# The experts' down projection in three fp32r products instead of plain f32

## The reference

```
for e in range(E):                                  # 8 experts
    g = xf @ wg[e].T                                # 256 -> 384
    u = xf @ wu[e].T                                # 256 -> 384
    y = jax.nn.silu(g) * u @ w_down[e].T            # 384 -> 256, "down"
    out = out + comb[:, e:e + 1] * y                # comb: 2 of 8 not zero
```

## Time and profile before

| | before |
|---|---|
| median of three runs | 576.96 us |
| span of the profiled execution (first to last instruction) | 575.3 us |
| PE, DVE, ACT, POOL busy | 482.2, 287.6, 204.3, 161.4 us |
| 39 tiles, from the fourth up block (385.66 us) to the last (534.82 us) | 149.16 us in 36 steps |

### The profile page before, as it was taken

How to read it: one execution, slowest core, us unless ns; L and a number is a source line. 1 busy time by engine, 2 the same in 40 slices (tenths; PEclk the granted TensorE clock), 3 DMA queues, 4 the chain that set the end, 5 groups by cost and what they waited for, 6 DMA issues and landing times.

```text
span 575.3 us, 9801 instructions
## 1 busy us (share of the span) xinstructions
PE 482.2 (84%) x2849; PEld 312.9 (54%) x2850; DVE 287.6 (50%) x590; ACT 204.3 (36%) x415; POOL 161.4 (28%) x186
## 2 busy tenths in 40 slices
PE   4536896999978997998879999279999999999890
PEld 2314442474424642473353555268888888888650
DVE  6746373647555572646544666114343433434357
ACT  1213464544536163544663444013232323232110
POOL 7004342312324043311211287601222222221200
PEclk9957799999979998998999999779999999999995
DMA  8759229191837539290207422212222222221168
GB/s 267 171 54 112 65 54 144 39 174 38 122 72 111 137 65 129 53 159 2 83 3 291 173 86 93 98 40 64 57 66 62 65 64 64 64 64 55 37 191 255
DMA packets 48193, 56.66 MB, mean 98 GB/s; under 512 B 10640, under 2 KB 43472, under 8 KB 47536
## 3 DMA queue, kind: packets, MB, share of 16 engines
q1 hardware_dynamic: 44768, 47.10, 38.0%
q0 software_dynamic: 3408, 9.34, 4.5%
HBM read 27.05 MB, written 16.59 MB: 76 GB/s over the span
## 4 chain that ended last, share of the span: by engine, by line
PE 53%; DMA 12%; DVE 9%; issue 7%; ACT 7%; POOL 6%; SPq 5%; ACTq 0%; POOLq 0%; DVEq 0%
PE set_b L889 9%; DMA attention<-attention 7%; POOL x_by_slot L555 6%; PE set_a L873 6%; PE set_a L592 5%; PE set_a L875 5%; PE set_a L874 5%; PE set_b L622 5%; SPq L357 5%; ACT attention L987 4%; PE set_a L643 3%; PE set_b L612 3%; DVE attention L1190 3%; PE set_a L798 2%; PE set_b L881 2%
## 5 line engine op out<-in xcount | busy, mean ns | idle before, releaser
L1190 DVE TENSOR_REDUCE attention<-set_a 128x2 f32<-128x1024 f32 (+2 forms) x96 | 96.7, 1042 | 57.5 <-PE set_a L594 55.6
L987 ACT ACTIVATE attention<-set_b 128x512 f32<-128x512 f32 (+1 forms) x176 | 87.5, 565 | 69.4 <-PE set_b L612 68.7
L592 PE MATMUL set_a<-attention 96*128 96x512 bf16 (+3 forms) x256 | 67.8, 330 | 32.7 <-DMA attention<-attention 26.0
L564 POOL DMA_INDIRECT y_by_choice<-moe,e_dst x39 | 37.2, 955 | 140.4 <-DVE moe L1372 131.8
L521 POOL TENSOR_SCALAR_AFFINE_SELECT attention<-attention 128x512 f32<-128x512 f32 x64 | 39.8, 634 | 116.3 <-ACT attention L987 116.2
L592 PEld LDWEIGHTS set_a<-attention 96*128 96x128 bf16 x256 | 26.7, 104 | 80.1 <-issue 46.2
L612 PE MATMUL set_b<-attention 99*128 99x512 bf16 (+3 forms) x256 | 60.8, 312 | 11.0 <-ACT attention L987 6.0
L1358 DVE TENSOR_TENSOR moe<-set_a,moe 128x384 f32<-128x384 f32 x39 | 21.7, 557 | 92.0 <-ACT moe L1075 92.0
L889 PE MATMUL set_b<-w_down,moe 128*128 x234 | 60.3, 388 | 1.1 <-DVE moe L1372 1.1
L1075 ACT ACTIVATE moe<-set_a 128x384 f32<-128x384 f32 x39 | 19.1, 490 | 116.7 <-PE set_a L875 116.7
L873 PE MATMUL set_a<-wup_hi,e_xT_hi 128*128 x156 | 57.1, 366 | 1.6 <-DVE e_xT_lo L1353 1.2
(11 more groups left out here) (152 smaller groups left out, 691.3 us busy)
## 6 DMA issues: line engine op xcount, KB each, us to landing
attention<-attention SPq DMA_DIRECT2D x96, 128.0 KB, 5.7
wup<-in_wupT SPq DMA_DIRECT2D x2, 3072.0 KB, 14.1
x_by_slot<-attention SPq DMA_DIRECT2D x13, 387.0 KB, 7.4
moe<-x_by_slot SPq DMA_DIRECT2D x39, 128.0 KB, 2.0
moe<-y_by_choice SPq DMA_DIRECT2D x16, 256.0 KB, 3.8
attention<-in_ctxT SPq DMA_DIRECT2D x7, 512.0 KB, 5.9
w_down<-in_wdnT SPq DMA_DIRECT2D x3, 1024.0 KB, 8.6
x_res<-in_x SPq DMA_DIRECT2D x4, 512.0 KB, 7.2
```

The costliest lines, as they stand in the source:

```text
L592: mm(dst, qstack[0:ROWS, g // 2, h, k * P:w], kstack[0:ROWS, g // 2, h, 0:w], start=True, stop=False)
L987: nc.scalar.activation(pT[k][:, h:h + heads, :], bank(par)[:, 0:heads * (S - k * P)], ACT.Exp).then_inc(b_free, 1)
L1190: v.tensor_reduce(dst, src, AX.X, ALU.max, negate=True).then_inc(a_free, 1)
```

## The change

Both operands of the down projection are split into a high part (a copy to fp32r) and a low part (the rest, in fp32r), and each f32 product becomes three fp32r products. The low part of the weights takes the place of the f32 weights in memory, the high part stands where the attention's buffers were. The weights are split once, after the third shared batch; the hidden rows in every step, where DVE gets a new instruction `hidden_lo`. `e_hTr`, for which PE waits, is now raised by DVE.

```
-        wdn = sb("w_down", [P, M, E * D])
+        with nc.sbuf_tensor("w_down", [P, M, E * D], F32) as wdn:
+            pass
+        wdn_lo = sb("w_down_lo", [P, M, E * D], F32R)
...
+        wdn_hi = sb("w_down_hi", [P, M, E * D], F32R)
...
                 for m in range(M):
-                    last = mm(Bk[:, 2, 0:D], e_hT[:, a, m, :], wdn[:, m, bass.ds(e * D, D)],
-                              start=m == 0, stop=m == M - 1)
+                    cols = bass.ds(e * D, D)
+                    dst = Bk[:, 2, 0:D]
+                    mm(dst, e_hT_hi[:, a, m, :], wdn_hi[:, m, cols], start=m == 0, stop=False)
+                    mm(dst, e_hT_hi[:, a, m, :], wdn_lo[:, m, cols], start=False, stop=False)
+                    last = mm(dst, e_hT_lo[:, a, m, :], wdn_hi[:, m, cols], start=False, stop=m == M - 1)
...
+            pe.wait_ge(dn_lo, M)
...
# ACT, after the last silu of the third shared batch
+            for m in range(M):
+                copy(wdn_hi[:, m, :], wdn[:, m, :]).then_inc(dn_hi, 1)
...
-                copy(e_hT[:, a], Bk[:, 1, 0:M * P].rearrange("p (c n) -> p c n", c=M)).then_inc(e_hTr, 1)
+                copy(e_hT_hi[:, a], Bk[:, 1, 0:M * P].rearrange("p (c n) -> p c n", c=M)).then_inc(e_hThi, 1)
...
# DVE
+            for m in range(M):
+                dve.wait_ge(dn_hi, m + 1)
+                v.tensor_tensor(wdn_lo[:, m, :], wdn[:, m, :], wdn_hi[:, m, :], ALU.subtract).then_inc(dn_lo, 1)
+
+            def hidden_lo(t, a):
+                dve.wait_ge(e_hThi, t + 1)
+                v.tensor_tensor(e_hT_lo[:, a], Bk[:, 1, 0:M * P].rearrange("p (c n) -> p c n", c=M),
+                                e_hT_hi[:, a], ALU.subtract).then_inc(e_hTr, 1)
...
             hidden(1, 1)
+            hidden_lo(0, 0)
             rows_lo(2, 0)
...
                 t = 2 * i + 1
+                hidden_lo(t, 1)
                 rows_lo(t + 2, 1)
                 result(t - 1, 0, i, wait)
                 hidden(t + 2, 1)
+                hidden_lo(t + 1, 0)
                 rows_lo(t + 3, 0)
...
+            hidden_lo(NT - 2, 1)
             result(NT - 3, 0, (NT - 3) // 2)
+            hidden_lo(NT - 1, 0)
...
-    nc = bacc.Bacc("TRN2", target_bir_lowering=False, num_devices=1)
+    nc = bacc.Bacc("TRN2", target_bir_lowering=False, num_devices=1, dynamic_dma_scratch_size=4096)
```

More of the change, by code:

```diff
@@ L125, in build @@
         MOE = 39 * KB
+        with nc.sbuf_tensor("e_hT_hi", [P, 2, M, P], F32R) as e_hT_hi, \
+                nc.sbuf_tensor("e_hT_lo", [P, 2, M, P], F32R) as e_hT_lo:
+            pass
         moe = sb("moe", [P, MOE])
@@ L194, in build @@
         parts_of(moe, C * N)
+        part(2 * 2 * M * P)
         e_x = part(2 * D).rearrange("p (a d) -> p a d", a=2)
@@ L197, in build @@
         e_h = part(2 * HALF).rearrange("p (a d) -> p a d", a=2)
-        e_hT = part(2 * M * P).rearrange("p (a c n) -> p a c n", a=2, c=M)
         e_y = part(2 * D).rearrange("p (a d) -> p a d", a=2)
@@ L253, in build @@
         up_hi, up_lo, wts_ready, e_xhi = (sem(n) for n in ("up_hi", "up_lo", "wts_ready", "e_xhi"))
-        e_xt, e_xTr, e_up, e_sgr, e_hr, e_ht, e_hTr, e_yf, e_yr = (sem(n) for n in
-            ("e_xt", "e_xTr", "e_up", "e_sgr", "e_hr", "e_ht", "e_hTr", "e_yf", "e_yr"))
+        e_xt, e_xTr, e_up, e_sgr, e_hr, e_ht, e_hThi, e_hTr, e_yf, e_yr = (sem(n) for n in
+            ("e_xt", "e_xTr", "e_up", "e_sgr", "e_hr", "e_ht", "e_hThi", "e_hTr", "e_yf", "e_yr"))
+        dn_hi, dn_lo = sem("dn_hi"), sem("dn_lo")
         y_in = [sem(f"y_in{i}") for i in range(NYB)]
```

## The result

| | before | after |
|---|---|---|
| median (range), beside each other | 576.74 us (576.19 to 578.29) | 591.0 us (590.55 to 592.43) |
| span of the profiled execution | 575.3 us | 590.7 us |
| PE, DVE, ACT, POOL busy | 482.2, 287.6, 204.3, 161.4 us | 481.0, 307.3, 209.7, 163.7 us |

The ratio of after to before is 1.0242, with a 95% interval of 1.0218 to 1.0265: slower by 2.4%. The forecast was 590.0 us.

What follows compares the result with a forecast made beforehand. DVE's `e_xT_lo`, not PE, was taken to set each up block's start. 11.0 us in the loop and 2.1 in the scatter on a span of 575.3 make 588.4, with 1.7 to the median 590.0 us; range 585 to 596.

Steps and rivals of the forecast that it cites:

- the larger term: Expert loop: `hidden_lo` on DVE delays each up block by 0.30 us, 11.0 us of the 13.1 added.
- What bounds the loop: Expert loop: DVE's `e_xT_lo` sets the up block's start, 0.14 us after its end; the down block is hidden.
- Part 1: Down block: nine fp32r products at 0.12 take 1.08 us, 0.22 less than now; hidden, so the gain is 0.
- Part 2: DVE in each step: `hidden_lo` ahead of `rows_lo` adds 0.30 us, 37 times: 11.0 us, at most 16.9.
- Part 3: Splitting the weights: hidden for ACT and DVE, but DVE's subtractions slow POOL's scatter by 2.1 us (1.6 to 2.65).
- full blocking: Skill's rule, not adopted: three new DVE pieces would hold POOL up to 6.8 us, some 5 above the term.
- Part 4: The rest: smaller descriptor memory costs 0, or 66 us if only one DMA fits; clock's mean effect 0.
- One sign of the list: Expert loop, if right: a window of PE about 86% busy, with a wait on DVE before the up block.
- PE's stream sets the loop: Rival: the up block waits for the down block, 39 blocks save 0.22 us each; 570.5 us, faster; chance 0.06.
- The rival with more exposed: DVE's instructions do not overlap (16.9), PE's sequencer is late (1.8), scatter pays 2.65: 21.4 us, 598; chance 0.10.
- that with less: Rival: something in a step gives back half of the 0.30; 5.5 + 2.1 makes 584.5 us; chance 0.07.
- mostly not: Scatter: +0.40 us per POOL DMA beside DVE pieces of 1.69 was read as mostly not full blocking.

Runs made afterwards that it cites:

- e4: Changed kernel without `hidden_lo`, with three high by high products in the down block in place of nine: 582.17 us, ratio 1.007.
- e2: Kernel before, f32 products kept, with `hidden_lo` alone added on DVE and PE's wait moved to it: 586.53 us, ratio 1.0158.
- e9: Kernel before with the rows of tile t + 2 taken first on PE, ACT and DVE, f32 products kept: 570.51 us, ratio 0.9875.
- e3: Changed kernel without `hidden_lo`, all nine products kept, the third reading the high hidden rows: 583.46 us, ratio 1.0086.
- e7: Changed kernel with one swap on DVE, `rows_lo` ahead of `hidden_lo`: 582.73 us, ratio 1.0108.
- e8: Changed kernel with the rows of tile t + 2 first on PE, ACT and DVE, and descriptor memory 8192: 574.23 us, ratio 0.9937.
- e5: Changed kernel with descriptor memory of 8192 in place of 4096: 592.66 us, ratio 1.0246.
- e6: e5 without DVE's subtractions for the low down weights, the middle product reading the high weights: 587.9 us, one run.
- e1: Kernel before with the descriptor memory alone cut to 4096: 580.02 us, ratio 1.0029.
- e11: e9 with the split of the up weights in 16 pieces of 768 instead of 8 of 1536: 568.76 us, ratio 0.9846.
- e10: e5 with DVE's subtraction for the low down weights in six pieces of 1024 instead of three of 2048: 592.53 us, ratio 1.0245.

## Why the prediction was right

The prediction gave 590.0 us, 13.1 of them added; 591.0 was measured, 14.3 more than before. The mechanism of the larger term is shown. That the total is within 1 us is in part luck, as the sum below shows. By its own parts:

- **What bounds the loop: shown.** The constant 0.14 behind `e_xT_lo`, in steps whose down blocks end at different times, was the reason. It held after (443.30 to 443.44), with three products (e4) and with f32 products (e2), and over all 37 up blocks of each. It went when the order made PE's stream the later one (e9), and in every second step of the kernels with nine products and an earlier `e_xT_lo` (e3, e7, e8).
- **Part 1: right.** The fp32r pitch is 0.118 where 0.12 was taken, the block 1.07 for 1.08, and it gives nothing back. e4 shows that a block of 0.36 gives nothing back either. The later start of the third group was there: 1.24 after the block's first load (446.06 to 447.30) where it was 1.05 before, 0.19 for the 0.25 forecast, and it cost nothing, since all steps after are 4.40. The slack was small, as the prediction said: with `e_xT_lo` back in its old place the nine products lengthen every second step (e3).
- **Part 2: right, slightly large.** +0.26 a step, not +0.30; 9.4 us over the loop's 38 intervals, not 11.0. From the start of `hidden` to the end of `e_xT_lo` it is 1.35 (441.95 to 443.30) where 1.38 was forecast: the neighbouring DVE instructions overlap by 0.08 and 0.09 where 0.08 was taken, and two records are 0.01 shorter (0.55 and 0.41). 37 x 0.30 is 11.1, not 11.0. e2 gives the term alone: a step of 4.404, and 586.53 us.
- **Part 3: right in place and sign, mis-sized.** Taken was 2.1 (at most 2.65); the subtractions alone cost 4.0 (e5 less e6). The 0.40 per DMA of the earlier trace rows belongs to pieces of 1536. For pieces of 2048 it is 1.90 - 0.96 = 0.94, and the DMA caught by the first piece takes 3.06, 2.1 more: 2.1 + 2 x 0.94 = 4.0. The prediction had read the 0.40 as a mild contention and dismissed the full blocking that would have made its term larger; the runs are on the side of blocking, piece by piece, as the section on the hardware shows.
- **Part 4: the descriptor memory was not free.** 4096 holds 28 of these scatters, and the 29th waits until the 28th has landed. Alone this is 2.1 us (e1). The prediction had 0, with an end of 66 that supposes one at a time. In the profile after it adds but 0.4 to part 3, in e3, e4 and e7 1.0 to 1.3. Parts 3 and 4 together: 4.4 where 2.1 was forecast. The clock stayed at 1.00, as taken.
- **The sum.** 9.4 + 4.4 + 0.5 + 1.1 (1.2 less 0.1) = 15.4 of span against 13.1. The loop was 1.6 too dear and the scatter 2.3 too cheap, two errors that mostly cancel: that is the luck. The two ends of the program, 1.6 together, were not forecast; they are about what the profiled execution is longer than the others of its kernel (1.5 to 2.1).

One sign of the list was wrong: PE was to be about 86% busy in the loop, and the window has 147.30 / 158.40 = 93%. The idle time is near the forecast of 0.6: by its pitches PE's stream is 3.70 of 4.40, which leaves 0.7. But matmul records run past the distance to the next, and cover the first part of a gap; the gap is read from the loads' starts.

Of the rivals, "PE's stream sets the loop" (570.5) is excluded by e2 and e4. It had a true core: the f32 stream is the next bound, 0.2 us below the first (e9). The rival with more exposed (598) fell on the overlap, that with less (584.5) on e2's full 0.26.

What stays open: why DVE's last addition of the third shared batch (L1308) began 1.7 us late in the profile after, which put the subtractions at 367.10 and not at 365.0 as in e5. Nor is the 1.2 us behind the last up block explained, nor what PE's sequencer does in the late third group.

## What to carry to other kernels

Before work is taken from an engine that is busy 100% of a stage, measure from several steps what its next block starts behind: a constant distance behind another engine's instruction (0.14 in each step here), and a varying one behind its own work, name the bound. New work on the engine that sets the pace belongs behind the instruction for which others wait: `hidden_lo` ahead of `rows_lo` cost 0.26 us a step, behind it at most 0.05, and sending the rows first on all engines gained 1.25% with the arithmetic left alone, where the change of arithmetic had lost 2.4%. A pass over weights that is hidden for its own engine may still be paid by GpSimd's DMAs beside it.

## What the runs showed of the hardware

**GpSimd's DMAs beside a DVE pass with both inputs in SBUF fall into step with DVE's pieces.** The distance from start to start of POOL's indirect DMAs against that of DVE's pieces:

| columns of a DVE piece | DVE, a piece | POOL, a DMA | pieces to a DMA |
|---|---|---|---|
| none | | 1.26 | |
| 768 (e11) | 0.87 | 1.74 | 2 |
| 1024 (e10) | 1.13 | 2.28 | 2 |
| 1536 | 1.67 | 1.66 | 1 |
| 2048 (e5) | 2.20 | 2.20 | 1 |

In these four sizes POOL's distance is a whole number of pieces, the least that exceeds its own 1.26. The ends show how: over all 14 traces, the 103 scatter DMAs that POOL starts while a piece runs and another follows end 0.90 to 0.93 us after the start of the next piece, whatever the size, and the 30 beside the last piece of a pass 0.83 to 0.84 after its end. Only the eight that POOL starts within 0.03 of the pass's beginning take their usual 0.96. In e5 the second and third piece start at 367.22 and 369.43, and the DMAs end at 365.08 + 3.06 = 368.14 and 368.44 + 1.90 = 370.34. In e10 the second and fourth start at 368.19 and 370.46, and the DMAs end at 369.10 and 371.37; the one started at 369.40 had just missed the piece of 369.32. So POOL stands until the boundary of two pieces and does nearly all of its own 0.96 behind it. The DMA caught by the first piece pays up to the whole of it (2.1 in e5), which makes long pieces dear in another way. That pieces a little above 1.26 cost least per DMA follows from this, and only the 1536 is measured. The Trainium skill ("SBUF — State Buffer", Who interferes with whom) has this pair blocking each other fully, the second until the first ends. The table and the ends agree, taken piece by piece, and the prediction's "mostly not" was wrong.

**The 0.118 of an fp32r product.** 256 columns at 2.4 GHz are 0.107 us, and each of these products loads 128 columns of its own over all 128 rows; a load that waited for the matmul would not fit. The rule of the Trainium skill ("TensorE: Matmul & The Clock Gate", What overlaps and what doesn't), by which such a load overlaps only for other rows of the array, does not hold for this stream.

**Descriptor memory is a budget.** With 4096 POOL issues 28 scatters of 128 rows, and the 29th starts only 0.84 us after the 28th has landed (e1, e3, e4), in e1 2.1 us beyond its pitch; with 8192 there was no pause within the 32. The pause has no releaser in the trace ("issue"), so it looks like any slow start.

**Once the matmuls are short, something between PE's instructions is the bound, by exclusion its sequencer:** in e8 every second down block takes 1.52 instead of 1.12, in e3 and e7 every second step is longer too, and the fp32r kernel (3.969 a step) ends behind the f32 one (3.943) whose products take more of PE's time.
